# A state-space mixer with a binarized feed-forward: weight scratch in fp8, weight loads cast on POOL's queue, two transposes moved into the scan

## What is computed

```python
x = x + LN(ssm(LN(x)))          # mixer
x = x + LN(ffn(LN(x)))          # feed-forward
# ssm: Bu = einsum('blh,pht->blpt', x, B_mat); a linear recurrence of 2x2 matrices along l for
#      each of P = 256 modes and both parts t; y = C_0 ys_0 - C_1 ys_1 + x * D_vec
# ffn: h = gelu(x @ (a1*sign(w1)).T + b1); out = h @ (a2*sign(w2)).T + b2
#      w1 is [4096, 1024], w2 [1024, 4096]; a1, a2: the mean of |w| over each row
```

## Time and profile before

| | |
|---|---|
| median of 3 runs | 3979.45 us (3975.87 to 4116.02) |
| profiled execution | 3974.94 us |
| its span, slowest core | 3973.2 us |
| spans of the 8 cores | 3928.5 to 3973.2 us |
| TensorE matmul / VectorE / ScalarE / POOL busy | 58% / 34% / 35% / 2% |
| HBM read / written | 608.27 / 67.11 MB |

### The profile page before, as it was taken

One profiled execution on the slowest core, in us unless ns is written; L12 is line 12 of the kernel. 1 busy time (PEld: TensorE's weight loads), 2 busy tenths in 40 slices (PEclk: granted clock), 3 DMA queues, 4 the chain that ended last, 5 costly groups with the idle time before them and its releaser, 6 DMA issues.

```text
span 3973.2 us, 43966 instructions; the slowest of 8 cores (3928.5 to 3973.2 us)
## 1 busy us (share of the span) xinstructions
PE 2293.2 (58%) x14408; PEld 1429.8 (36%) x14408; DVE 1366.6 (34%) x3058; ACT 1403.0 (35%) x2135; POOL 92.4 (2%) x156
## 2 busy tenths in 40 slices
PE   0000035848485766667574848485766667584866
PEld 0000013525253444444342525253444444352544
DVE  1024055161615243333425161615243333425031
ACT  4530023333434342424333343434342424343343
POOL 0000100000000000000000000000000000000000
PEclk9997557879788888888797979797888888797988
DMA  6687432818273644546371717273645546372744
GB/s 191 208 174 168 116 127 85 270 57 277 73 250 123 209 172 180 201 154 228 115 266 68 276 62 280 78 263 118 215 167 180 201 154 227 113 269 73 266 156 183
DMA packets 177520, 695.02 MB, mean 175 GB/s; under 512 B 78568, under 2 KB 78734, under 8 KB 110480
## 3 DMA queue, kind: packets, MB, share of 16 engines
q1 hardware_dynamic: 151312, 591.53, 44.9%
q0 software_dynamic: 25984, 100.67, 7.2%
HBM read 608.27 MB, written 67.11 MB: 170 GB/s over the span
## 4 chain that ended last, share of the span: by engine, by line
PE 42%; DVE 19%; DMA 16%; issue 11%; ACT 11%; DVEq 1%; ACTq 0%; SPq 0%; POOLq 0%; POOL 0%
PE pb L908 19%; PE pcA L925 11%; PE pcB L925 10%; DMA w2s<-scr_w2t 5%; DVE sx L813 2%; DVE u L712 2%; ACT tt L810 2%; DMA scr_w2b<-n1tm 2%; DMA scr_w1b<-n1tm 1%; ACT junk L817 1%; ACT junk L644 1%; DMA outb<-w 1%; DVE ys L724 1%; DVE u L722 1%; DVE dtm L683 1%
## 5 line engine op out<-in xcount | busy, mean ns | idle before, releaser
L908 PE MATMUL pb<-n2fm,w1s 128*128 128x256 bf16 x8192 | 1110.6, 282 | 303.7 <-DVE n2fm L852 303.7
L908 PEld LDWEIGHTS pb<-n2fm,w1s 128*128 128x128 bf16 x8192 | 826.5, 101 | 643.8 <-issue 331.6
L915 ACT ACTIVATE gel<-pb,b1col,a1col 128x256 bf16<-128x256 f32 x1024 | 574.7, 564 | 1259.7 <-PE pb L908 1259.3
L925 PE MATMUL pcA<-w2s,gel 128*128 128x512 bf16 x2048 | 632.6, 392 | 332.7 <-ACT gel L915 297.5
L925 PE MATMUL pcB<-w2s,gel 128*128 128x512 bf16 x2048 | 629.9, 390 | 0.0
L925 PEld LDWEIGHTS pcA<-w2s,gel 128*128 128x128 bf16 x2048 | 196.9, 99 | 386.2 <-issue 361.6
L949 DVE TENSOR_TENSOR mo<-pcA,b2rep 128x1024 f32<-128x1024 f32 x16 | 19.6, 1225 | 888.0 <-PE pcA L925 888.0
L925 PEld LDWEIGHTS pcB<-w2s,gel 128*128 128x128 bf16 x2048 | 205.4, 100 | 259.0 <-issue 30.1
L967 DVE TENSOR_TENSOR amo<-pcA,b2rep 128x1024 f32<-128x1024 f32 x16 | 19.6, 1225 | 698.6 <-PE pcA L925 612.5
L674 PE MATMUL pt<-id,n1tm 128*128 128x128 bf16 x512 | 47.6, 267 | 334.6 <-DVE n1fm L678 314.1
L732 PE MATMUL pb<-n1fm,cB 128*128 128x512 bf16 x512 | 167.5, 500 | 66.1 <-DVE u L738 49.9
(11 more groups left out here) (294 smaller groups left out, 2298.3 us busy)
## 6 DMA issues: line engine op xcount, KB each, us to landing
w1s<-scr_w1t SPq DMA_DIRECT2D x256, 1024.0 KB, 6.2
w2s<-scr_w2t SPq DMA_DIRECT2D x256, 1024.0 KB, 6.9
sx<-x POOLq DMA_DIRECT2D x32, 1024.0 KB, 11.1
outb<-w SPq DMA_DIRECT2D x32, 512.0 KB, 4.6
tt<-w SPq DMA_DIRECT2D x32, 512.0 KB, 5.4
out<-outb POOLq DMA_DIRECT2D x32, 512.0 KB, 3.5
out<-amo POOLq DMA_DIRECT2D x32, 512.0 KB, 3.3
scr_w1b<-n1tm POOLq DMA_DIRECT2D x8, 1024.0 KB, 7.3
```

The costliest lines, as they stand in the source:

```text
L908: pe(lambda e, k=k, bk=bk, wr=wr, hbq=hbq, hf=hf: e.matmul(pb[bk][:, 0:256], w1s[wr][:, k * 512 + hbq * 128: k * 512 + hbq * 128 + 128], n ...
L915: act(lambda e, hb=hb, bk=bk, gs=gs: e.activation(gel[gs][:, :], pb[bk][:, 0:256], AF.Gelu, bias=b1col[:, hb:hb + 1], scale=a1col[:, hb:hb ...
L925: pe(lambda e, hb=hb, mg=mg, ng=ng, wr=wr, gs=gs, hbq=hbq: e.matmul(pcm[mg][:, ng * 512:(ng + 1) * 512], gel[gs][:, mg * 128:(mg + 1) * 12 ...
```

## The change

The transposed weight scratch becomes fp8 (signs are exact in it). SBUF tiles stay bf16, so the scratch writes and all weight loads cast on the way, and the loads move from SP's queue to POOL's. The w1s ring has two tiles in place of three, and its loads are written one piece later. As a2 no longer goes into the signs of w2, its column goes through DRAM (scr_a) into a row that two matmuls spread over all partitions (a2rep), and both evacuations of a pass multiply by it before b2rep is added. `t3_one(u, 0)`, `ln2_apply(u, 3)` and `t3_one(u, 1)` move into `bu_scan` of the next unit.

```diff
+FP8 = mybir.dt.float8e4
...
-    s_w1t = nc.dram_tensor("scr_w1t", [8, 128, HF], BF16, kind="Internal").ap()
-    s_w2t = nc.dram_tensor("scr_w2t", [8, 128, 4 * H], BF16, kind="Internal").ap()
+    s_w1t = nc.dram_tensor("scr_w1t", [8, 128, HF], FP8, kind="Internal").ap()
+    s_w2t = nc.dram_tensor("scr_w2t", [8, 128, 4 * H], FP8, kind="Internal").ap()
+    s_a2 = nc.dram_tensor("scr_a2", [8, 128], F32, kind="Internal").ap()
...
+        a2rep = sb("a2rep", [128, H], F32)
...
-        w1s = [sb(f"w1s{r}", [128, 8 * 512], BF16) for r in range(3)]
+        w1s = [sb(f"w1s{r}", [128, 8 * 512], BF16) for r in range(2)]
...
+        a2col = sb("a2col", [128, 8], F32)
...
-            dve(lambda e: e.tensor_scalar(n1tm[:, :], n1tm[:, :], st3[:, 4:5], None, ALU.mult, ALU.bypass),
-                reads=["n1tm", "st3.q"], writes=["n1tm"])
+            dve(lambda e, chunk=chunk: e.tensor_copy(a2col[:, chunk:chunk + 1], st3[:, 4:5]),
+                reads=["st3.q"], writes=["a2col"])
...
+
+        for chunk in range(8):
+            dma("gp", lambda e, chunk=chunk: e.dma_start(out=s_a2[chunk, :], in_=a2col[:, chunk]),
+                reads=["a2col"], writes=["s_a2"], sem="dws")
+        dma("sp", lambda e: e.dma_start(out=amo[1][0:1, :], in_=s_a2.rearrange("c p -> (c p)")[None, :]),
+            reads=["s_a2"], writes=["amo1"], sem="dp")
+        dve(lambda e: e.memset(outb[1][0:1, 128:256], 1.0), writes=["outb1"])
+        pe(lambda e: e.matmul(pcm[0][:, 0:512], outb[1][0:1, 128:256], amo[1][0:1, 0:512], start=True, stop=True),
+           reads=["outb1", "amo1"], writes=[PCM[0][0]])
+        pe(lambda e: e.matmul(pcm[0][:, 512:1024], outb[1][0:1, 128:256], amo[1][0:1, 512:1024], start=True, stop=True),
+           reads=["outb1", "amo1"], writes=[PCM[0][1]])
+        dve(lambda e: e.tensor_copy(a2rep[:, :], pcm[0][:, :]), reads=[PCM[0][0], PCM[0][1]], writes=["a2rep"])
         def emit_table(Cd, Bd, cresC, cresB, sres, sres2, colw, basen, ncols):
...
-        def bu_scan(u):
+        def bu_scan(u, t3u=None):
             def scan_tail(b):
...
+                if t3u is not None and b == 1:
+                    t3_one(t3u, 0)
+                    _, _, xres_t, xtiles_t = unit_tiles(t3u)
+                    ln2_apply(t3u, 3, xres_t, xtiles_t)
+                if t3u is not None and b == 2:
+                    t3_one(t3u, 1)
...
         def emit_w1_load(g):
-            piece, wr = g % 8, g % 3
-            dma("sp", lambda e, piece=piece, wr=wr: e.dma_start(
+            piece, wr = g % 8, g % 2
+            dma("gp", lambda e, piece=piece, wr=wr: e.dma_start(
...
-            dma("sp", lambda e, piece=piece, wr2=wr2: e.dma_start(
+            dma("gp", lambda e, piece=piece, wr2=wr2: e.dma_start(
...
                 def ffn1(hb):
-                    wr = (gbase + piece) % 3
+                    wr = (gbase + piece) % 2
...
                     if (hb - 1) % 4 == 3:
-                        emit_w1_load(gbase + (hb - 1) // 4 + 3)
+                        emit_w1_load(gbase + (hb - 1) // 4 + 2)
                 ffn2(31)
-                emit_w1_load(gbase + 10)
+                emit_w1_load(gbase + 9)
-                        dve(lambda e, mg=mg: e.tensor_tensor(mo[mg][:, 0:H], pcm[mg][:, :], b2rep[:, :], ALU.add),
-                            reads=[PCM[mg][0], PCM[mg][1], "b2rep"], writes=[f"mo{mg}"])
+                        dve(lambda e, mg=mg: e.tensor_tensor(mo[mg][:, 0:H], pcm[mg][:, :], a2rep[:, :], ALU.mult),
+                            reads=[PCM[mg][0], PCM[mg][1], "a2rep"], writes=[f"mo{mg}"])
+                        dve(lambda e, mg=mg: e.tensor_tensor(mo[mg][:, 0:H], mo[mg][:, 0:H], b2rep[:, :], ALU.add),
+                            reads=[f"mo{mg}", "b2rep"], writes=[f"mo{mg}"])
...
         def evac_h1(u):
-                dve(lambda e, mg=mg: e.tensor_tensor(amo[mg][:, :], pcm[mg][:, :], b2rep[:, :], ALU.add),
-                    reads=[PCM[mg][0], PCM[mg][1], "b2rep"], writes=[f"amo{mg}"])
+                dve(lambda e, mg=mg: e.tensor_tensor(amo[mg][:, :], pcm[mg][:, :], a2rep[:, :], ALU.mult),
+                    reads=[PCM[mg][0], PCM[mg][1], "a2rep"], writes=[f"amo{mg}"])
+                dve(lambda e, mg=mg: e.tensor_tensor(amo[mg][:, :], amo[mg][:, :], b2rep[:, :], ALU.add),
+                    reads=[f"amo{mg}", "b2rep"], writes=[f"amo{mg}"])
         def tail_h1(u):
...
-        emit_w1_load(2)
...
             if u + 1 < NU:
-                bu_scan(u + 1)
+                bu_scan(u + 1, t3u=u)
-            t3_one(u, 0)
-            _, _, xres_u, xtiles_u = unit_tiles(u)
-            ln2_apply(u, 3, xres_u, xtiles_u)
-            t3_one(u, 1)
+            else:
+                t3_one(u, 0)
+                _, _, xres_u, xtiles_u = unit_tiles(u)
+                ln2_apply(u, 3, xres_u, xtiles_u)
+                t3_one(u, 1)
             if u >= 1:
```

## The result

The changed kernel takes 4315.56 us (median of 9 runs) against 3980.93 us; the ratio is 1.085 (95% interval 1.0817 to 1.0883). Predicted were 4347 us and slower by over 2%; the range of 4220 to 4950 us holds the time. The profiled execution took 4314.47 us, span 4312.9 us, on core 1.

What follows compares the result with a forecast made beforehand. The prediction took TensorE to bound the feed-forward pass and VectorE the mixer stretch, with late work at the seams costing full length. It summed 208 + 77 + 87 + 0 + 0 = 372 us on 3974.9 to 4347 us, range 4220 to 4950.

Steps and rivals of the forecast that it cites:

- The x loads behind the weights: End of each pass: late x loads hold VectorE's sums and the evacuation, 14.85 us for 14 units, +208 us.
- the landing of x: End of a pass: second x load lands 13.5 us after T0, the end of the last matmul, at 314 GB/s.
- The multiplies: Both evacuations of a pass: two added 1226 ns VectorE operations each, nearly all uncovered, +77 us.
- The setup: Before the first unit: VectorE's tables wait for the a2rep copy, +98 less 11 us, together +87 us.
- the price of one write of 128 four-byte elements: Setup, scr_a writes: 3.5 us each, 28 us for eight in a row, bounds 12 to 32.
- two things that I had at 0 and -11: Setup: transposed scratch writes, half the bytes but cast, 0; scaling of n1tm leaving seven chunks' path, -11 us.
- The moved transposes: Start of each pass: the n2fm wait goes but the gelu wait behind it grows, 0; bound -303.7 us.
- The weight loads: Loads in the pass, now on POOL: landing stays under 7.8 us, TensorE keeps pace, 0; bounds -35 to +317 us.
- Rival 1: Weight loads in the pass: casting loads are slow and bind it, 4664 us, or some 5590; chance 0.30.
- the two terms at 0: The forecast's terms for the moved transposes and for the weight loads themselves, each put at 0 us.

Runs made afterwards that it cites:

- e1: Changed kernel with the x loads issued right behind the stores of half 0, ahead of half 1's weight loads; 4124.62 us, ratio 1.036.
- e5: Changed kernel with both transposed scratch tensors back in bf16, so no casts, loads still on POOL's queue; 4405.79 us, ratio 1.0983, comparison unclear.
- e9: Changed kernel without the multiplies by a2rep, so the scale of w2 is left out (time only); 4258.4 us, ratio 1.0617.
- e3: Changed kernel with a2rep made on the chip by VectorE and matmuls with ones, without scr_a; 4187.0 us, ratio 1.0533.
- e4: Changed kernel with the two transposes and the last apply put back behind the scans, ahead of the pass; 4354.47 us, ratio 1.0932.
- e7: Kernel before with layer-norm tails in steps inside the next half, x loads in mid half 1, transposes moved into the next scan; 3646.6 us, ratio 0.9107.
- e8: Changed kernel with x loads back behind the stores of half 0 and a2rep made on the chip; 3971.15 us, ratio 0.9964.

## Why the prediction was right, and where its terms were off

**The x loads behind the weights: +208 forecast, 195 measured** (e1 on core 7; 191 by the medians). The mechanism is the one described, and e1 takes it out. The evacuation came at T0+14.4 in the pass shown, at T0+14.7 in the mean of core 7 (13.6 to 15.4), where T0+16.2 was forecast. By the step's own terms: 14.6 us of shift less the 1.25 us is 13.35 us a unit, not 14.85; e1 gives 13.9. The mis-sized part is the landing of x. The second load landed at T0+11.7, not T0+13.5. With bf16 loads in the same order (e5) it lands at T0+12.6 to T0+14.0, by core, so the forecast fitted weight loads that read 1 MB and not ones that read half of it. The 1.7 us of latency inside the 13.5 stand in no row. And the step followed the wrong load: it counts two sums from the landing of the second, but the four sums run without a gap from the landing of the first (T0+9.2). Had only the second come sooner, the evacuation would have stayed where it is. That both ways of counting end within some 0.2 us of each other is chance. The estimate from the Trainium skill ("DMA: Bandwidth & Descriptors", "Anatomy of one DMA — SWDGE (gpsimd) path") put the second load at T0+10. It landed at T0+11.7, half way between that estimate and my T0+13.5.

**The multiplies: +77 forecast, 79 measured** (e9: 4.95 us a unit for four operations of 1.22 us each).

**The setup: +87 forecast, +106 on core 7** (92 to 128 over the eight cores; 118 from slowest core to slowest). The order was right: the tables start behind the scr_a chain. The step that failed is the price of one write of 128 four-byte elements: I took 3.5 us "between" two rows, with 12 to 32 us as bounds of the eight; they took 72 us. Neither bounding row was of this kind: the 256 KB write of the earlier trace rows has long runs of bytes, and this one takes one element from each of 128 partitions. That the shape makes it slow is an inference; no run writes the same bytes in another shape. Against that stood two things that I had at 0 and -11: on core 7 the last write of w2's transposed scratch was issued at 471.5, where the earlier trace rows has 507.48. e5, with bf16 scratch, has it at 499.4, so fp8 gives 28 of these 36 us; the other 8 fit the multiply that went out of n1tm. The sum hid this: e3 shows that the chain costs 149 us and the rest of the setup's change gives 44 back. At the first statistics e5 gives only 21 of the 44 to fp8 on core 7 (32 in the mean of the cores); the remainder was not tried apart.

**The moved transposes: 0 forecast, 0 in the steady state, some -13 at unit 0.** Rows 9 were read rightly: e4's intervals are those of the changed kernel. The wait for n2fm did not go to nothing, 53.5 of 303.7 us stay. I read one pass in the middle and did not ask which unit lacks the thing that is late next. e7 shows the other side: with the tails out of the way the same move takes 172 us.

**The weight loads: 0 forecast, -35.** Rival 1 (slow casting loads, 0.30) is out: they land in 4.7 and 5.0 us. The 34.7 us of w2s waits went, which I had only as the lower bound. My reason for 0, "by the row of the same transfer without the cast", took the bytes written to be what counts; e5 shows that the size of the source counts.

Sum of what was measured, on core 7: 195 + 79 + 106 - 13 - 35 = 332 us; the span of that core grew by 324.5, so the terms are 8 us too many. The same terms without x and with e8's setup (39 us before that of the kernel before) give 79 - 39 - 13 - 35 = -8 us for e8, where core 7's spans differ by -19 and the medians by -10. The forecast's 372 is 40 above the sum: x too high by 13, the two terms at 0 too high by 48, against the setup too low by 19 and the multiplies by 2. Errors of both signs brought 4347 within 31 us of the median. That closeness is luck: the chain of eight writes alone was wrong by 44 us.

## What to carry to other kernels

When a load is moved onto a queue that others share, list what else stands on it in program order: a late x load in front of an in-order engine cost more here (195 us) than halved weight traffic gave (about 80). Small DMAs on one semaphore cost their time one after another (72 us for eight here, 19 on semaphores of their own), so give each its own, or make the row on the chip. And a wait that looks like the gain is one only if nothing behind it is late at the same moment; look for the stretch (here unit 0) where that second thing is missing, and for the edit that removes both.

## What was not expected of the hardware

A casting load from fp8 in HBM to 1 MB of bf16 in SBUF lands in 4.7 and 5.0 us (medians of the changed kernel); the same 1 MB without the cast takes 6.1 to 6.9 us, from either queue (e5 and the earlier trace rows). A write of 128 elements of 4 bytes, one from each partition, takes 7.5 to 9.1 us from issue to the next issue behind it, and 13.8 us for the first, which is issued 0.6 us after a larger scratch write; eight at once take 19.4 us until the load behind them. And one core's granted clock was 0.80 to 0.81 in its early passes (e4) where the changed kernel's was 0.95 to 0.98 in the same place, for no reason that these traces show.
